# Attention's value products in two blocks of 256 columns instead of one of 512, with score tiles and a unit of maxima between the blocks

## The reference

```python
q = _lin(_lin(x, wq_w, wq_b), vq_w, vq_b)      # k and v alike
scores = jnp.einsum('cbqh,cbkh->cbqk', q, k) / scale
attn = jax.nn.softmax(scores, axis=-1)
o = jnp.einsum('cbqk,cbkh->cbqh', attn, v)
x = _layernorm(x + _lin(o, wo_w, wo_b))
x = _layernorm(x + _L0_xattn_ref(x, ctx_1024, fside_BxSx1_0, ...))   # a convolution with gates
x = _layernorm(x + _L0_ffn_ref(x, ...))
```

## Time and profile before

| | |
|---|---|
| runs (3) | median 2124.9 us, 2123.53 to 2125.03 |
| span of the profiled execution | 2122.5 us |
| PE busy | 2067.2 us (97%) |
| DVE busy | 1659.3 us (78%) |
| ACT busy | 1314.4 us (62%), in the attention about 81% |
| granted TensorE clock in the attention | 1.00, the level of 2.4 GHz |
| attention's steps | 512, about 2.62 us each |

### The profile page before, as it was taken

One profiled execution on the slowest core, in us unless ns is written; L12 is line 12 of the kernel. 1 busy time (PEld: TensorE's weight loads), 2 busy tenths in 40 slices (PEclk: granted clock), 3 DMA queues, 4 the chain that ended last, 5 costly groups with the idle time before them and its releaser, 6 DMA issues.

```text
span 2122.5 us, 39702 instructions
## 1 busy us (share of the span) xinstructions
PE 2067.2 (97%) x11249; PEld 1165.3 (55%) x11264; DVE 1659.3 (78%) x1727; ACT 1314.4 (62%) x2429; POOL 491.5 (23%) x878
## 2 busy tenths in 40 slices
PE   9999999999999999999999999999999999988996
PEld 4788775444444444444444444444444387767874
DVE  4333356888899999999999998999898576886687
ACT  0112113778888888888888888888888742454344
POOL 0000001121212221221122122212121371465245
PEclk9999998999999999999999999999999999999997
DMA  4456735555575665664665646655647578773672
GB/s 164 139 159 155 186 112 109 84 123 137 100 139 120 108 136 97 131 143 95 135 128 101 141 103 123 137 99 126 138 99 179 182 267 306 278 254 124 222 262 101
DMA packets 214414, 315.25 MB, mean 149 GB/s; under 512 B 105424, under 2 KB 121808, under 8 KB 202064
## 3 DMA queue, kind: packets, MB, share of 16 engines
q1 hardware_dynamic: 214352, 314.47, 58.9%
HBM read 211.06 MB, written 101.19 MB: 147 GB/s over the span
## 4 chain that ended last, share of the span: by engine, by line
PE 86%; DVE 6%; ACT 2%; SPq 2%; DMA 2%; issue 1%; POOL 1%; DVEq 0%; POOLq 0%; ACTq 0%
PE psum L542 26%; PE psum L551 23%; PE psum L187 22%; PE psum L223 11%; PE psum L88 2%; DVE stats L1392 1%; ACT probs L616 1%; DVE y L1517 1%; PE psum L1312 1%; DVE gates L1491 1%; DVE gates L1488 1%; SPq L208 1%; ACT gates L1241 1%; DVE y L1422 0%; DMA x_block<-in_x_t_dram 0%
## 5 line engine op out<-in xcount | busy, mean ns | idle before, releaser
L230 DVE TENSOR_REDUCE neg_max<-psum 128x1 f32<-128x1024 f32 x1024 | 1206.0, 1220 | 135.2 <-PE psum L223 135.0
L616 ACT ACTIVATE probs<-psum 128x512 f32<-128x512 f32 x2048 | 1065.3, 606 | 273.5 <-PE psum L542 269.3
L542 PE MATMUL psum<-q_op,k_op 50*128 50x512 f32 x2048 | 750.3, 449 | 3.9 <-ACT probs L616 1.4
L542 PEld LDWEIGHTS psum<-q_op,k_op 50*128 50x128 f32 x2048 | 353.6, 191 | 580.2 <-ACT probs L616 565.3
L223 PE MATMUL psum<-k_op,q_op 48*128 48x512 f32 x2048 | 620.2, 479 | 1.0 <-DVE neg_max L230 1.0
L551 PE MATMUL psum<-probs,v_op 128*32 128x512 f32 x4096 | 548.1, 607 | 5.8 <-ACT probs L616 2.9
L223 PEld LDWEIGHTS psum<-k_op,q_op 48*128 48x128 f32 x2048 | 389.0, 315 | 21.1 <-issue 4.4
L187 PE MATMUL psum<-x_wino,conv_w 128*128 128x512 f32 x1152 | 276.0, 395 | 1.0 <-DMA conv_w<-conv_w_parts_dram 1.0
L187 PEld LDWEIGHTS psum<-x_wino,conv_w 128*128 128x128 f32 x1152 | 214.4, 188 | 47.0 <-issue 1.3
L241 POOL CAST neg_max_parts<-neg_max 128x8 fp32r<-128x8 f32 x128 | 24.5, 191 | 887.8 <-DVE neg_max L230 887.8
L551 PEld LDWEIGHTS psum<-probs,v_op 128*32 128x32 f32 x4096 | 82.5, 108 | 136.8 <-ACT probs L616 70.0
(11 more groups left out here) (103 smaller groups left out, 1629.8 us busy)
## 6 DMA issues: line engine op xcount, KB each, us to landing
q_op<-qk_parts_dram SPq DMA_DIRECT2D x384, 128.0 KB, 4.1
conv_w<-conv_w_parts_dram SPq DMA_DIRECT2D x32, 1536.0 KB, 6.9
qk_parts_dram<-qk_parts SPq DMA_DIRECT2D x128, 256.0 KB, 3.2
k_op<-qk_parts_dram SPq DMA_DIRECT2D x384, 64.0 KB, 4.0
conv_w_parts_dram<-conv_w_parts SPq DMA_DIRECT2D x16, 1536.0 KB, 6.1
attended_dram<-out SPq DMA_DIRECT2D x64, 256.0 KB, 2.2
attended_parts_dram<-o_parts SPq DMA_DIRECT2D x128, 128.0 KB, 2.5
gates<-in_ctx_dram SPq DMA_DIRECT2D x32, 512.0 KB, 7.7
```

What stands on the lines that cost most here:

```text
L230: nc.vector.tensor_reduce(ops["max"][b][:, t:t + 1], mem["pair"][t % 2][:], AX_X, ALU.max, negate=True).then_inc(ops["maxed"], 1)
L542: nc.tensor.matmul(score_bank(i, n, j, last), kop[i][r, j // 2, n // 2 * P:(n // 2 + 1) * P], qop[i][r, j // 2, j % 2 * HALF:(j % 2 + 1) * ...
L616: nc.scalar.activation(probs[n % DEEP][:, j, :], score_bank(k, n, j, last), ACT.Exp, scale=SCALE).then_inc(exp_done, 1)
```

## The change

Each value product of 512 columns becomes two of 256: columns 0 to 255 in a first block of four matmuls, columns 256 to 511 in a second. The order of a step becomes: tile, unit, tile, tile, **first block**, unit, tile, **second block**. Both blocks are still those of step n - 1. The wait for bank 7 (`pv_out`) stands before the first block. The order of tiles in odd steps is swapped in pairs so that lanes alternate in the same way in every step; ScalarE takes them in that order.

```diff
-            def pv(s, k, n):
-
-                pe.wait_ge(exp_done, s * (STEPS * TILES) + n * TILES + TILES + RING)
+            def values(s, k, n, half):
+
+                if n == 0 and half == 0:
+                    pe.wait_ge(v_ready, s + 1)
+                    pe.wait_ge(pv_out, s + 1)
+                if half == 0:
+                    pe.wait_ge(exp_done, s * (STEPS * TILES) + n * TILES + TILES + RING)
+                cols = slice(half * (HALF // 2), (half + 1) * (HALF // 2))
                 for j in range(TILES):
                     kt = n // 2 + QT // 2 * ((n + j) % 2)
-                    mm = nc.tensor.matmul(pv_bank[32 * j:32 * j + 32, :], vop[k % 2][:, j // 2 * QT + kt, :],
-                                          probs[n % DEEP][:, j, :], start=(n == 0), stop=(n == STEPS - 1))
-                mm.then_inc(pv_step, 1)
+                    mm = nc.tensor.matmul(pv_bank[32 * j:32 * j + 32, cols], vop[k % 2][:, j // 2 * QT + kt, :],
+                                          probs[n % DEEP][:, j, cols], start=(n == 0 and half == 0),
+                                          stop=(n == STEPS - 1), skip_group_check=True)
+                if half == 1:
+                    mm.then_inc(pv_step, 1)
...
                 for n in range(STEPS):
...
+                    t, u = n * TILES, 2 * n
+                    shifted(it, k, t, last)
+                    unit(it, k, u, 1, last)
+                    shifted(it, k, t + 1, last)
+                    shifted(it, k, t + 2, last)
+                    values_before(n, 0)
+                    unit(it, k, u + 1, 0, last)
+                    shifted(it, k, t + 3, last)
+                    values_before(n, 1)
...
-            pv(LAST * 4 + 3, 3, STEPS - 1)
+            for half in range(2):
+                values(LAST * 4 + 3, 3, STEPS - 1, half)
...
-                        for j in range(TILES):
-                            act.wait_ge(s2_full, s * (STEPS * TILES) + n * TILES + j + 1)
-                            nc.scalar.activation(probs[n % DEEP][:, j, :], score_bank(k, n, j, last), ACT.Exp,
+                        for c in range(TILES):
+                            t = n * TILES + c
+                            act.wait_ge(s2_full, s * (STEPS * TILES) + t + 1)
+                            nc.scalar.activation(probs[n % DEEP][:, c ^ n % 2, :], score_bank(k, t, last), ACT.Exp,
                                                  scale=SCALE).then_inc(exp_done, 1)
-                            if n == 1 and j == 0 and not (first and k == 0):
+                            if t == TILES and not (first and k == 0):
                                 evacuate(s - 1, (k - 1) % 4, it * 2 + (k - 1) // 2)
```

More of the change, by code:

```diff
@@ L444, in load_taps, with score_bank @@
                 .then_inc(taps_in, DMA)
-        def score_bank(k, n, j, last):
-            wide = (k * STEPS + n - WIDE_FROM) * TILES + j
+        def score_bank(k, t, last):
+            cell = k * (STEPS * TILES) + t
+            wide = cell - WIDE_FROM * TILES
             if last and wide >= 0:
                 return wide_bank[wide % (2 * RING)]
-            return s2_bank[(k * (STEPS * TILES) + n * TILES + j) % RING]
+            return s2_bank[cell % RING]
         @block.sync
@@ L529, in _, with shifted @@
             pe.wait_ge(v_out, 4 + PROJECTED // 3)
[L531 to L534, removed]
+            def shifted(it, k, t, last):
+                n, c = t // TILES, t % TILES
+                j = c ^ n % 2
+                r = slice(LANE * (t % 2), LANE * (t % 2) + ROWS_SHIFT)
+                cell = k * (STEPS * TILES) + t
+                wide = cell - WIDE_FROM * TILES
+                if n == 0 and c % 2 == 0:
+                    pe.wait_ge(max_in[k][j // 2], (it + 1) * MAXES + DMA)
                 if last and RING <= wide < 2 * RING:
@@ L538, in s2 @@
                 elif last and wide >= 2 * RING:
-                    pe.wait_ge(exp_done, ready - RING)
+                    pe.wait_ge(exp_done, it * 4 * (STEPS * TILES) + cell + 1 - RING)
                 else:
-                    pe.wait_ge(exp_done, ready)
-                nc.tensor.matmul(score_bank(i, n, j, last), kop[i][r, j // 2, n // 2 * P:(n // 2 + 1) * P],
-                                 qop[i][r, j // 2, j % 2 * HALF:(j % 2 + 1) * HALF],
+                    pe.wait_ge(exp_done, it * 4 * (STEPS * TILES) + cell + (2 if cell < 2 else 1))
@@ L544, in s2, with unit @@
+                nc.tensor.matmul(score_bank(k, t, last), kop[k][r, j // 2, n // 2 * P:(n // 2 + 1) * P],
+                                 qop[k][r, j // 2, j % 2 * HALF:(j % 2 + 1) * HALF],
                                  start=True, stop=True).then_inc(s2_full, 1)
-            def pv(s, k, n):
-                pe.wait_ge(exp_done, s * (STEPS * TILES) + n * TILES + TILES + RING)
+            def unit(it, k, u, lane, last):
+                s = it * 4 + k
+                ahead = k + 1 if u < QT else k + 2
+                if last and ahead >= 4:
+                    return
+                if u == QT:
+                    pe.wait_ge(op_in[ahead % 4], (it + ahead // 4 + 1) * OPS)
+                pe.wait_ge(maxed, s * 16 + u + LEAD - 1)
+                b, t = 1 - u // QT, u % QT
+                score_lane(nc, mem, ops, ahead % 4, b, t, lane)
+                score_lane(nc, mem, ops, ahead % 4, b, t, 1 - lane).then_inc(s1_full, 1)
@@ L553, in pv @@
-                mm.then_inc(pv_step, 1)
+                    mm = nc.tensor.matmul(pv_bank[32 * j:32 * j + 32, cols], vop[k % 2][:, j // 2 * QT + kt, :],
[3 more added lines that the diff above has]
+                    mm.then_inc(pv_step, 1)
             def slot(it, k, first=False, last=False):
                 s = it * 4 + k
-                for n in range(STEPS):
[L558 to L583, removed]
@@ new lines, in values_before @@
+                def values_before(n, half):
+                    if n > 0:
+                        values(s, k, n - 1, half)
+                    elif not (first and k == 0):
+                        values(s - 1, (k - 1) % 4, STEPS - 1, half)
+                for n in range(STEPS):
+                    t, u = n * TILES, 2 * n
[7 more added lines that the diff above has]
+                    values_before(n, 1)
```

## The result

The changed kernel takes 3252.1 us (median of 4 runs, 3251.47 to 3253.89) against 2124.58 us before: ratio 1.531, 95% interval 1.529 to 1.533. I had forecast 2295 us, in a range of 2205 to 2365. The direction was right and the size was wrong by a factor of more than six.

The account below looks back on a forecast made before the run. A ring of latencies between TensorE and ScalarE, no full engine, was taken to set the 2.61 us step. 2122.5 + 125 (longer steps) + 43 (bank wait) + 2 (steps without units) = 2292.5, forecast 2295 us, range 2205 to 2365.

Parts of the forecast that it names:

- the first paragraph's clock: TensorE's granted clock, read from the profile page as 0.9 to 1.0 throughout, that is 2.4 GHz.
- the extra passages and the odd tile: Per step on TensorE: second handover into and out of value products, about 0.43 us, and unpartnered tile, 0.12 to 0.24.
- the stall: TensorE's fourth tile waits for the first tile's exponential to free a bank; the change removes this, 0.37 us a step.
- unit to second block: Step's second part on TensorE, unit and fourth tile before the second block: 0.78 to 0.90 us, taken as 0.84.
- step 1 of a slot, beyond that: First block waits for ScalarE's copy from 0.90 to 1.68 us after the tile, 0.78 us longer than neighbouring steps.
- step without units: The last 12 steps, which have no units: 2.20 us each, 0.2 us more than before, +2 us in all.
- The emptied bank: Step 1's first value block waits for ScalarE's copy, 0.68 us more than before, over 63 copies: +43 us.
- 1 (the switch nearly free): TensorE overlaps second handover and lone tile: step 2.24, kernel 1983 us; chance 0.03 in full, 0.04 partly faster, 0.03 no change.
- 2 (the wait covered): Step 1's bank wait is hidden by a late step before: 2252 us; with a cheap block, 2160 to 2250, chance 0.13.
- 3 (latency between short sets): Value blocks take 0.77 us, latency paid between sets: +215, 2510 us, or 2400 at half; chance 0.12, mostly at half.
- 4: ScalarE becomes the bound, with four exponentials at 2.0 us a step and the copy's 0.5 in eight steps; no chance given.
- I count nothing for the issue: Eight more matmul records and eight more weight loads a step on TensorE were taken to cost nothing.

Follow-up runs that it names:

- the new order written out: Changed kernel with the old order in slots 0 to 3 and TensorE's loop over slots 4 to 59 unrolled: 2268.6 us, ratio 1.069 to the kernel before.
- moving the copy: Changed kernel, old order in slots 0 to 3, TensorE's loop unrolled, ScalarE's copy of bank 7 ahead of step 1's first exponential: 2724.9 us.
- side by side blocks: Kernel before with its value products as two 256-column blocks directly behind each other at the step's end: 2252.7 us; with TensorE's loop unrolled 2162.9 us.
- the old slots: Slots 32 and 33, the only ones in the old order in a changed kernel with TensorE's loop unrolled: 2747.9 us.
- blocks together in step 1: Changed kernel, old order in slots 0 to 3, later slots' step 1 with both blocks at its end: 2648.7 us; TensorE's loop unrolled 2518.4 us.
- two tiles each: Changed kernel reordered so that each 256-column block stands behind tile, unit, tile, with no tile alone: 2733.8 us.
- the last run: Changed kernel, its loop kept, with the old order in slots 0 to 3 and in the first slot of every four after: 2472.0 us.
- the first run: Changed kernel with the old order in slots 0 to 3 and the new one from slot 4 on, loop kept: 3137.7 us.

## Why the prediction was wrong

**What failed is the first paragraph's clock**: "at a granted clock of 0.9 to 1.0 throughout, that is 2.4 GHz", taken as given for the changed kernel. Every term of the sum was worked out at that clock, and no rival let it go. The reading was wrong as well: the line of 40 slices has an 8 in its seventh slice (318 to 371 us), and that 8 is the fall of 13.6 us at the very start of the attention, which the view of windows shows. What the runs showed in its place: 2475 us of the attention at 0.50, and 4.77 us for a step forecast at 2.86. A rival "the thinner stream does not win the clock back" could have been priced from rows of before: there a step at 0.50 took 4.12 us (350.40 to 354.52) against 2.61.

```profile
350.40 0.79 PE L542 MATMUL psum<-q_op,k_op 50*128 50x512 f32 x1
352.66 1.94 PE L551 MATMUL psum<-probs,v_op 128*32 128x512 f32 x8
354.52 0.79 PE L542 MATMUL psum<-q_op,k_op 50*128 50x512 f32 x1
```

An estimate from these rows: to the 4.12 us add the 0.62 us that the prediction's sum puts on the extra passages and the odd tile (0.25 and the 0.37 of the stall), about 4.7 us. That is some 2.1 us more a step than 2.61, and 2125 + 500 x 2.1 = 3175 us.

**The steps of the sum themselves held**, at the clock for which they were made (the new order written out at 1.00):

| step of the prediction | forecast | measured at 1.00 |
|---|---|---|
| tile to first block | 0.90 us | 0.91 |
| a block of 256 columns | 0.56 us | 0.56 to 0.57 |
| unit to second block | 0.84 us | 0.79 to 0.80 |
| whole step | 2.86 us | 2.83 |
| step 1 of a slot, beyond that | 0.78 us | 0.81 |
| step without units | 2.20 us | 2.22 |
| the kernel | 2295 us | 2268.6 (4 slots in the old order, loop written out) |

So the prediction is right that the stall goes, and that a second handover and an odd tile cost more than it: without any trouble of clock the change, in that form, still makes the kernel 6.9% slower. "The emptied bank" is shown by moving the copy. Of the rivals, 1 (the switch nearly free) is wrong, since the step is 2.83; 2 (the wait covered) is wrong; 3 (latency between short sets) is wrong, since side by side blocks leave the step at 2.62; 4 did not come up.

**"I count nothing for the issue" was wrong as well**, hidden behind the larger error. The eight more records a step (and as many loads of weights) make the loop's body too long to stay fetched. Where that stood alone it cost 9 to 10 us a turn. In the changed kernel at 1.2 GHz the profile puts 11.2 us of matmul idle to it over the whole span, so it is small there; its weight is that such a gap is a place where the clock falls.

**Shown, and what stays open.** Shown: the new order runs at two clocks, 2.83 and 4.77 us a step; the same code runs at either; the old order brings the high one back, within 5 us in one run and seven times in another. Shown too: once low, the new order stayed low for 2475, 2192 and 1246 us to the end of the attention and for 1235 us to the old slots, in four runs, while variants that keep a denser stretch (blocks together in step 1, two tiles each) got out by themselves after 7 to 416 us.

What goes ahead of a fall is shown as well. Behind the start of the attention the clock falls 88 times in the traces of eleven of these runs. Every one of the 88 falls begins while TensorE stands still, or at most 2.6 us after such a stop has ended: for the copy of bank 7 (0.65 to 1.04 us), for the maxima (0.51 us and more) or in a gap at the loop's jump. In the kernel before, where the score tiles' matmuls wait 3.9 us in all and those of the value products 5.8, there is none behind the start.

Not settled: when a stop is enough. The written-out run at full clock has a hold of 0.73 us or more in every slot and never falls, and 27 of 35 holds of 0.87 us or more passed without a fall in the last run; the first run and that written-out one, which part ways here, also ran on different chips. No fall came without a stop, and most stops brought no fall. That lone tiles are what makes the stream thin was argued, and the run with two tiles each bears it out in part only.

No version beat the kernel before.

## What to carry to other kernels

Read the clock in windows around every change of stage and wherever its line is not 9, and ask of each new order not only how long its step is at the clock of today but whether it would win that clock back from the low one; price the step at 1.2 GHz as a rival of its own. A stall that goes is worth nothing if more handovers and lone tiles cost more than it: count them from starts first. Count the instructions in a loop's body on the busiest engine before adding to it, and look at the number of instruction packets behind.

## What the runs showed that I had not expected

- The clock can stay at 1.2 GHz for 2475 us under a stream that the profile calls 97% busy, and two programs that differ in four slots and a loop differ by 980 us (3252.1 and 2268.6).
- Every fall of the clock inside the attention came during or just behind a stop of TensorE, and many of these stops were only 0.5 to 1 us long; most stops of that length brought none.
- A loop's body on TensorE stays fetched up to some length, read from the instruction packets of a run: 33 before, 36 with a body in which three slots of four are the new kind, 138 to 156 with all four, 104 with the old body doubled. Beyond it each turn cost 9 to 10 us, and straight code for the same work 0.8%.
- A block of float32 value products of 256 columns costs its passes and one handover: 0.56 us at 2.4 GHz and 1.01 at 1.2. Four passes of 256 columns are 0.43 and 0.85 us of that (an estimate from 1024 columns at either clock, as in the prediction), which leaves 0.13 to 0.16 us around the block.
